# Two attentions and two mixture layers on one core: late normalisation spread out, roots inside head 14's values, two prepared pieces further apart, GpSimd behind the first rows

## The chip, the cores and the metric

One core of one Trainium2 chip. The metric is the device time of one launch in microseconds; less is better.

## The reference, cut to what matters

The input x has 4 batches of 512 rows of 512 numbers. Four layers are added to it in turn, each on a normalised copy:

```python
x = x + attn_a(layernorm(x), w_in, w_out)          # 16 heads of 128, causal
x = x + ffn(layernorm(x), gate_w, w1, b1, w2, b2, shared...)   # 8 experts, top 2, and a shared one
x = x + attn_b(layernorm(x), Wqa, Wqb, Wkva, Wkvb, Wo)         # latent attention
x = x + ffn(layernorm(x), ...)

def layernorm(x): return (x - mean) / sqrt(var + 1e-5)
def attn_a(x, w_in, w_out):
    q, k, v = split(x @ w_in.T)                    # per head
    p = softmax(causal(q @ k.T / sqrt(128)))
    return concat_heads(p @ v) @ w_out.T
```

The change lies in the first line alone.

## The kernel before, in words

Every matrix product is done in three TensorE passes on a high part and a low part of both operands (`product`): ScalarE copies a value into its rounded high part, and VectorE or GpSimd subtracts that from the value to get the low part. So each tile goes TensorE, ScalarE, VectorE and back to TensorE.

The first attention runs in two passes (g = 0 with batches 0 and 1, g = 1 with batches 2 and 3), in each 16 heads h, in each head two steps i, one per batch. Each engine has its own instruction list in program order (`attend_tensor`, `attend_scalar`, `attend_vector`, `attend_gpsimd`, `attend_sync`) and waits on semaphores; there is no planner. `over_heads` writes head pair 0 and head pair 7 out and loops over pairs 1 to 6. A step is a pipeline over three (head, batch) units: it projects query, key and values of the present one, takes mask, maximum and exponentials of the one before (u) and turns and multiplies its probabilities, and adds the output of the one before that (v). Heads 1 to 14 (`not edge(h)`) form query and key of both batches from seven half products, m1 to m7, over sums of the inputs; heads 0 and 15 do them plainly. Both heads' values of a pair are projected together in the even head, in two halves (`project_v`, `values_hi`, `values_lo`), each half with its own PSUM bank, which m7 and m4 of the same step (or m1 and m6 of the next) need again.

What else is woven in:

- Input sums. At the beginning of a pass GpSimd rebuilds the plain inputs (`rebuild_first`, `rebuild_second`), VectorE and GpSimd form four sums (`input_sums`, `third_sum`), ScalarE rounds them (`sums_hi`) and VectorE and GpSimd take the low parts (`sums_lo`). Head 1's half products need them.
- Normalisation. Batch 0 is normalised ahead of the attention, batch 1 inside head 0 of pass 0 (`woven_first`: TensorE turns a tile, ScalarE and VectorE split it). Batches 2 and 3, and then batches 0 and 1 for the next layer, are the late batches (`late_batch`): they are measured in step 0 of head 14 (`measure`: four statistics, four aggregates and the variance for each batch, then five small Newton instructions for each), ScalarE takes the roots there (`roots`), GpSimd makes the rows, and head 15 turns them.
- Pieces. 24 blocks of weights of the later layers are split ahead of time (`prepare`): SP loads one, ScalarE makes the high part, GpSimd the low part, and SP waits for that and stores both. There is one buffer: the load of piece j waits until piece j - 1 is stored. `pieces_of` says in which step a piece is done; pieces 15 and 16 stand in the two steps of head 1 in pass 1, pieces 17 to 23 in the second step of each later even head.
- The SP queue in a head: the next head's query and key weights (after GpSimd has taken the low parts of the present ones), its output weights, in even heads the values' weights, then the head's pieces.

The functions that build the norm and hand `measure` to the attention stand in `program`, in the blocks of VectorE and ScalarE.

Of the kernel before, what the change touches and what calls it, by code (L numbers as in the profile page):

```python
# [314 lines left out]
def pieces_of(g, pair, odd, i):  # L315

    begins = isinstance(pair, int) and pair == 0
    if g == 0:
        return [2 * pair + odd - 1] if i and (odd or not begins) else []
    if begins:  # L320
        return [H - 1 + i] if odd else []
    return [H + pair] if i and not odd else []
# [328 lines left out]
def attend_scalar(nc, act, m, n, a, first=nothing, roots=nothing, prepare=nothing):  # L651
# [55 lines left out]

    def values_hi(g, h, i):
        for half in range(2):
            act.wait_ge(a.v_done, 2 * (H * g + h) + 2 * i + half + 1)  # L710
            for other in range(2):
                nc.scalar.activation(values_part(values_of(m, other, i)[HI], half), values_bank(m, half, other),  # L712
                                     ACT.Copy).then_inc(a.v_hi, 1)

    def sums_hi(g):
        act.wait_ge(a.x_summed, 6 * g + 2)
        nc.scalar.activation(sum_place(m, HI, g, 2), plain_sum(m, LO, g, 2), ACT.Copy).then_inc(a.sum_hi, 1)
        nc.scalar.activation(sum_place(m, HI, g, 1), plain_sum(m, LO, g, 1), ACT.Copy).then_inc(a.sum_hi, 1)
        act.wait_ge(a.x_summed, 6 * g + 3)
        nc.scalar.activation(sum_place(m, HI, g, 4), plain_sum(m, LO, g, 4), ACT.Copy).then_inc(a.sum_hi, 1)  # L720
        act.wait_ge(a.rebuilt, 6 * g + 5)
        nc.scalar.activation(sum_place(m, HI, g, 3), plain_sum(m, LO, g, 3), ACT.Copy).then_inc(a.sum_hi, 1)
# [6 lines left out]
    def step(g, pair, h, odd, i, n1, new=True, hook=nothing):  # L729
# [61 lines left out]
        if n1:  # L791
            output_hi(u)
        if new and not odd:
            values_hi(g, h, i)
        if new and edge(h) and not odd and g == 1 and i == 0:
            sums_hi(g)
        if new:
            for j in pieces_of(g, pair, odd, i):
                prepare(j)
        if new and i == 0 and isinstance(h, int) and h == H - 2:  # L800
            roots(g)
        hook(i, 3)
# [11 lines left out]

def attend_vector(nc, dve, m, n, a, first=nothing, measure=nothing):

# [107 lines left out]
    def step(g, h, odd, i, n1, n2, new=True, hook=nothing):  # L924
# [55 lines left out]
        elif not odd:  # L980
# [9 lines left out]
            if g == 0 and i:  # L990
                input_sums(g)
            add((2, 3))
        else:
# [11 lines left out]
        if new and edge(h) and not odd and g == 1 and i == 0:  # L1005
            input_sums(g)
        if new and edge(h) and not odd:
            values_lo(g, h, i, (0,))
            if i:
                sums_lo(g, (2, 1))  # L1010
            values_lo(g, h, i, (1,))
        elif new and not odd:
            values_lo(g, h, i, (0, 1))
        if new and i == 0 and isinstance(h, int) and h == H - 2:
            measure(g)
        hook(i, 3)
# [12 lines left out]
def attend_gpsimd(nc, pool, m, n, a, prepare=nothing, use_tables=nothing):  # L1029
# [47 lines left out]
    def rebuild_first(g):  # L1077
        if g:
            pool.wait_ge(a.proj_done, 4 * H * g)
        pool.wait_ge(n.xt_lo, NT * (2 * g + 1))  # L1080
        rebuild(g, plain_sum(m, HI, g, 3), 2 * g, 0)
        rebuild(g, plain_sum(m, HI, g, 4), 2 * g, 1)
# [6 lines left out]
    def third_sum(g):  # L1089
        pool.wait_ge(a.x_summed, 6 * g + 2)  # L1090
        pool.wait_ge(a.rebuilt, 6 * g + 4)
        third = plain_sum(m, LO, g, 3)
        nc.gpsimd.tensor_tensor(third, plain_sum(m, HI, g, 3), third, ALU.subtract).then_inc(a.rebuilt, 1)
        pool.wait_ge(a.sum_hi, 4 * g + 4)
        nc.gpsimd.tensor_tensor(sum_place(m, LO, g, 3), third, sum_place(m, HI, g, 3).bitcast(F32),
                                ALU.subtract).then_inc(a.rebuilt, 1)
# [10 lines left out]
    def head(g, pair, odd):  # L1107
# [23 lines left out]
        if edge(h) and not odd and g == 0:  # L1131
            third_sum(g)
        if odd and coming:
            rest_vw(*coming)
        if isinstance(h, int) and h == H - 2:
            late_rows(g, 0, (0, 1))
        for i in range(2):
            for j in pieces_of(g, pair, odd, i):
                prepare(j)

    rest_ahead(0, 0)
    rest_vw(0, 0)
# [1548 lines left out]
def program(nc, x_in, wa, wva, woa, wb, wob, rope, gate, b1, wr, b1r, b2r, b2s, table, out):  # L2691
    with ExitStack() as ctx:
# [117 lines left out]
        m.rank = sb("rank", [P, GT])  # L2810
        m.esc, m.first, m.ids = sb("esc", [P, TILES]), sb("first", [P, 2]), sb("ids", [P, IDS], U32)
        m.picked = [sb("picked0", [P, GT + 1, E], BF16), sb("picked1", [P, NT + 1, E], BF16)]
        m.tri16, m.ones16 = sb("tri16", [P, P], BF16), sb("ones16", [P, P], BF16)
# [102 lines left out]

        def woven_first(stats, start, tile):

            def first(b, i):
# [3 lines left out]
                for t in ((), (0,), (1, 2), (3,))[i] if b == 0 and i >= 0 else ():  # L2923
                    tile(1, t)
            return first

# [41 lines left out]
        def _(dve):  # L2968
# [28 lines left out]

            def measure(g):
                for i in range(2):
                    if g == 0:  # L3000
                        dve.wait_ge(x_loaded[2 + i], 16)
                    norm_measure_vector(nc, dve, m, n, *late_batch(g, i))
                for i in range(2):
                    norm_newton_vector(nc, dve, m, n, *late_batch(g, i))

            attend_vector(nc, dve, m, n, a1, woven_first(stats(0), start(0), tile(0)), measure)
            dve.wait_ge(small_loaded, SMALL)

# [118 lines left out]
```

## Time and profile before

| | us |
|---|---|
| median of three runs | 2427.64 (2424.67 to 2428.95) |
| the profiled execution | 2426.1 |
| its span | 2423.9 |
| TensorE busy in it | 2276.9 (94%) |
| VectorE busy | 1826.9 (75%) |
| ScalarE busy | 1206.4 (50%) |
| GpSimd busy | 935.8 (39%) |

The first attention takes the first 1055 us or so of the span. PE is TensorE, PEld its weight loads, DVE VectorE, ACT ScalarE, POOL GpSimd, SP the engine that issues the loads. A row of the timeline has start, duration, engine, line, operation, what is written and read, and, if the engine was idle before it, in brackets how long and what released it. PEclk is the TensorE clock granted in a stretch, as a share of 2.4 GHz: 1.00 is that level and 0.50 the lower one, 1.2 GHz.

### The profile page before, as it was taken

The numbers are of one execution on the slowest core, as the hardware profiler recorded it, in microseconds if no ns is written. First come the engines' busy times: TensorE is split into PE (matmuls) and PEld (weight loads), VectorE is DVE, ScalarE is ACT, GpSimd is POOL, SyncE is SP. The second block draws the span as 40 slices with busy tenths as digits, with TensorE's granted clock in tenths as the row PEclk, the third lists the DMA queues.
The fourth block names the chain that finished last, engine by engine and source line by source line (L and its number), as shares of the span: only waits on it lengthen the run. The fifth ranks groups of instructions, "written<-read, shape, count | busy, mean of one in ns | idle before, by whom it ended". The sixth has DMA issues, their size and how long they took to land. (4 is left out here: it accounts for less than half of the span.)

```text
span 2423.9 us, 41931 instructions
## 1 busy us (share of the span) xinstructions
PE 2276.9 (94%) x12798; PEld 1953.5 (81%) x12798; DVE 1826.9 (75%) x4044; ACT 1206.4 (50%) x2803; POOL 935.8 (39%) x757
## 2 busy tenths in 40 slices
PE   6999999989899999888999789999999999889997
PEld 5888888878788888767887568888888888767886
DVE  6877777767677777766666749999999999875666
ACT  3555555555455555542332446666666666542334
POOL 5444444365344444345221333333334334234223
PEclk9999999999999999999999899999999999999999
DMA  3455555532533333226884100000000000017866
GB/s 124 168 194 194 194 194 194 194 119 91 210 114 114 114 114 114 81 82 227 300 274 179 58 19 1 19 19 0 18 18 18 0 18 18 18 62 271 282 232 232
DMA packets 106768, 296.61 MB, mean 122 GB/s; under 512 B 9481, under 2 KB 11913, under 8 KB 101025
## 3 DMA queue, kind: packets, MB, share of 16 engines
q1 hardware_dynamic: 85792, 239.59, 28.4%
q0 software_dynamic: 11360, 37.76, 4.1%
q10 hardware_dynamic: 9504, 17.85, 2.2%
q8 instruction: 61, 1.00, 0.2%
q14 instruction: 51, 0.41, 0.1%
HBM read 150.18 MB, written 144.98 MB: 122 GB/s over the span
## 5 line engine op out<-in xcount | busy, mean ns | idle before, releaser
L74 PE MATMUL bank<-wo_hi,hq_hi 128*128 128x512 f32 x576 | 235.5, 409 | 14.7 <-DVE x L1439 13.0
L74 PE MATMUL bank<-xT_hi,w_hi 128*128 128x512 f32 x584 | 236.1, 404 | 10.8 <-DVE xT_lo L1693 4.3
L76 PE MATMUL bank<-xT_hi,w_lo 128*128 128x512 f32 x584 | 232.4, 398 | 0.0
L75 PE MATMUL bank<-xT_lo,w_hi 128*128 128x512 f32 x584 | 232.2, 398 | 0.0
L76 PE MATMUL bank<-wo_hi,hq_lo 128*128 128x512 f32 x576 | 226.6, 393 | 0.0
L75 PE MATMUL bank<-wo_lo,hq_hi 128*128 128x512 f32 x576 | 226.4, 393 | 0.0
L1509 POOL TENSOR_TENSOR qf<-ra,rb 64x512 f32<-64x512 f32 x64 | 82.4, 1287 | 334.1 <-DVE rb L1612 333.9
L831 DVE SCALAR_TENSOR_TENSOR x<-bank,inv,x 128x512 f32<-128x512 f32 x256 | 179.8, 743 | 19.8 <-PE bank L76 19.8
L1357 ACT ACTIVATE s<-s,top 128x128 f32<-128x128 f32 (+3 forms) x256 | 141.0, 552 | 96.6 <-DVE top L1431 96.4
L1439 DVE SCALAR_TENSOR_TENSOR x<-bank,inv,x 128x512 f32<-128x512 f32 x256 | 180.0, 743 | 3.7 <-PE bank L76 0.7
L842 DVE TENSOR_TENSOR hq_lo<-bank,hq_hi 128x512 fp32r<-128x512 f32 (+1 forms) x144 | 80.3, 567 | 130.1 <-ACT arena L712 67.2
L672 ACT ACTIVATE s<-s,top 128x128 f32<-128x128 f32 (+3 forms) x256 | 140.9, 552 | 56.8 <-DVE top L822 56.8
L1033 POOL TENSOR_TENSOR w_lo<-w_raw,w_hi 128x512 fp32r<-128x512 f32 x64 | 82.5, 1290 | 210.0 <-ACT w_hi L648 210.0
L74 PEld LDWEIGHTS bank<-wo_hi,hq_hi 128*128 128x128 f32 x576 | 109.2, 190 | 53.6 <-DVE x L1439 26.3
L74 PEld LDWEIGHTS bank<-xT_hi,w_hi 128*128 128x128 f32 x584 | 112.6, 193 | 37.6 <-DVE xT_lo L192 8.7
L76 PEld LDWEIGHTS bank<-xT_hi,w_lo 128*128 128x128 f32 x584 | 112.0, 192 | 24.5
L75 PEld LDWEIGHTS bank<-xT_lo,w_hi 128*128 128x128 f32 x584 | 112.3, 192 | 24.1
L76 PEld LDWEIGHTS bank<-wo_hi,hq_lo 128*128 128x128 f32 x576 | 109.0, 189 | 24.0
L838 DVE TENSOR_TENSOR pt_lo<-bank,pt_hi 128x384 fp32r<-128x384 f32 (+1 forms) x192 | 104.6, 594 | 31.0 <-ACT pt_hi L678 30.9
L76 PE MATMUL bank<-pt_hi,hq_lo 128*128 128x256 f32 (+2 forms) x384 | 124.6, 324 | 0.0
L75 PE MATMUL bank<-pt_lo,hq_hi 128*128 128x256 f32 (+2 forms) x384 | 124.3, 324 | 0.0
L74 PE MATMUL bank<-pt_hi,hq_hi 128*128 128x256 f32 (+2 forms) x384 | 124.1, 323 | 0.0
(338 smaller groups left out, 7315.9 us busy)
## 6 DMA issues: line engine op xcount, KB each, us to landing
sorted_x<-blank SPq DMA_DIRECT2D x48, 1584.0 KB, 11.6
arena<-split_w SPq DMA_DIRECT2D x32, 1024.0 KB, 5.8
split_w<-arena SPq DMA_DIRECT2D x48, 512.0 KB, 3.5
w_raw<-dram_wa SPq DMA_DIRECT2D x32, 512.0 KB, 5.0
raw<-dram_wr SPq DMA_DIRECT2D x24, 512.0 KB, 5.6
wo_raw<-dram_woa SPq DMA_DIRECT2D x32, 256.0 KB, 4.2
ctok<-dram_wva SPq DMA_DIRECT2D x16, 512.0 KB, 5.1
arrived<-routed_y SPq DMA_DIRECT2D x8, 1024.0 KB, 8.0
```

What stands on the lines that cost most here:

```text
L74: nc.tensor.matmul(out, hi, mov_hi, start=first, stop=False)
L75: nc.tensor.matmul(out, hi, mov_lo, start=False, stop=False)
L76: return nc.tensor.matmul(out, lo, mov_hi, start=False, stop=last)
L672: nc.scalar.activation(at, at, ACT.Exp, bias=m.top[:, slot, t:t + 1], scale=-1.0, accum_out=m.rowsum[:, slot, t:t + 1]).then_inc(a.probs_r ...
L831: nc.vector.scalar_tensor_tensor(out=xt, in0=m.bank[6 + t % 2][:, :], scalar=m.inv[:, slot, t:t + 1], in1=xt, op0=ALU.mult, op1=ALU.add).t ...
L838: nc.vector.tensor_tensor(m.pt_lo[:, dst:dst + cols], m.bank[src][:, 0:cols], m.pt_hi[:, dst:dst + cols].bitcast(F32), ALU.subtract).then_ ...
L842: return nc.vector.tensor_tensor(out, whole, hi.bitcast(F32), ALU.subtract).then_inc(done, 1)
L1033: nc.gpsimd.tensor_tensor(lo, whole, hi.bitcast(F32), ALU.subtract).then_inc(a.w_lo, 1)
L1357: nc.scalar.activation(at, at, ACT.Exp, bias=m.top[:, odd, t:t + 1], scale=-1.0, accum_out=m.rowsum[:, odd, t:t + 1]).then_inc(a.probs_rea ...
L1439: nc.vector.scalar_tensor_tensor(out=xt, in0=m.bank[6 + t % 2][:, :], scalar=m.inv[:, odd, t:t + 1], in1=xt, op0=ALU.mult, op1=ALU.add).th ...
L1509: nc.gpsimd.tensor_tensor(m.qf[HALF:P, :], m.ra[HALF:P, :], m.rb[HALF:P, :], ALU.add).then_inc(a.rope_added, 1)
```

## The change

It moves work between places in the program and adds two waits and one small instruction:

- In each pass one late batch is measured in head 0 (in pass 0 in step 0, in pass 1 in step 1), only the other in head 14.
- In step 0 of head 14 ScalarE takes the roots ahead of the first half of the values, and a one-column exponential between the halves; VectorE does the first Newton step and the other measurement ahead of the values and the second Newton step between their halves.
- The third sum's rounding (`third_hi`) goes behind the values of step 1 of head 0, its low part (`third_lo`) on GpSimd behind the next head's weights. In pass 0 VectorE takes the low part of the second sum earlier, and that of the first behind the values.
- Piece 15 goes from head 1 to step 1 of head 0.
- GpSimd waits for the first two rows of batch 0 before its first weights and for the first two of batch 1 before its first rebuild.

```diff
@@ pieces_of
     if begins:
-        return [H - 1 + i] if odd else []
+        return [H - 1 + odd] if i else []
@@ attend_scalar
-    def values_hi(g, h, i):
-        for half in range(2):
-            act.wait_ge(a.v_done, 2 * (H * g + h) + 2 * i + half + 1)
-            for other in range(2):
-                nc.scalar.activation(values_part(values_of(m, other, i)[HI], half), values_bank(m, half, other),
-                                     ACT.Copy).then_inc(a.v_hi, 1)
+    def values_hi(g, h, i, half):
+        act.wait_ge(a.v_done, 2 * (H * g + h) + 2 * i + half + 1)
+        for other in range(2):
+            nc.scalar.activation(values_part(values_of(m, other, i)[HI], half), values_bank(m, half, other),
+                                 ACT.Copy).then_inc(a.v_hi, 1)
...
+    def third_hi(g):
         act.wait_ge(a.rebuilt, 6 * g + 5)
         nc.scalar.activation(sum_place(m, HI, g, 3), plain_sum(m, LO, g, 3), ACT.Copy).then_inc(a.sum_hi, 1)
...
+        before_last = new and i == 0 and isinstance(h, int) and h == H - 2
+        if before_last:
+            roots(g)
         if new and not odd:
-            values_hi(g, h, i)
+            values_hi(g, h, i, 0)
+            if before_last:
+                nc.scalar.activation(m.exp_set[:, 0:1], m.root[:, 0, 0:1], ACT.Exp)
+            values_hi(g, h, i, 1)
         if new and edge(h) and not odd and g == 1 and i == 0:
             sums_hi(g)
+        if new and edge(h) and not odd and i:
+            third_hi(g)
         if new:
             for j in pieces_of(g, pair, odd, i):
                 prepare(j)
-        if new and i == 0 and isinstance(h, int) and h == H - 2:
-            roots(g)
@@ attend_vector
             if g == 0 and i:
                 input_sums(g)
+                sums_lo(g, (2,))
+            if g == 1 and i:
+                dve.wait_ge(a.y_added, NT * (v + 1) - NT)
+                measure(g, 0)
             add((2, 3))
...
-        if new and edge(h) and not odd:
+        before_last = new and i == 0 and isinstance(h, int) and h == H - 2
+        if before_last:
+            newton(g, 0)
+            measure(g, 1)
+        if new and not odd:
             values_lo(g, h, i, (0,))
-            if i:
+            if edge(h) and i and g:
                 sums_lo(g, (2, 1))
+            if before_last:
+                newton(g, 1)
             values_lo(g, h, i, (1,))
-        elif new and not odd:
-            values_lo(g, h, i, (0, 1))
-        if new and i == 0 and isinstance(h, int) and h == H - 2:
-            measure(g)
+            if edge(h) and i and not g:
+                sums_lo(g, (1,))
@@ attend_gpsimd
     def rebuild_first(g):
         if g:
             pool.wait_ge(a.proj_done, 4 * H * g)
+        else:
+            pool.wait_ge(n.normed, NT + 2)
         pool.wait_ge(n.xt_lo, NT * (2 * g + 1))
...
+    def third_lo(g):
+        third = plain_sum(m, LO, g, 3)
         pool.wait_ge(a.sum_hi, 4 * g + 4)
...
         if edge(h) and not odd and g == 0:
             third_sum(g)
+        if edge(h) and not odd:
+            third_lo(g)
         if odd and coming:
             rest_vw(*coming)
...
+    pool.wait_ge(n.normed, 2)
     rest_ahead(0, 0)
     rest_vw(0, 0)
     use_tables()
@@ program, woven_first
                 for t in ((), (0,), (1, 2), (3,))[i] if b == 0 and i >= 0 else ():
                     tile(1, t)
+                if b == 0 and i == 1:
+                    measured()
@@ program, VectorE's block
-            def measure(g):
-                for i in range(2):
-                    if g == 0:
-                        dve.wait_ge(x_loaded[2 + i], 16)
-                    norm_measure_vector(nc, dve, m, n, *late_batch(g, i))
-                for i in range(2):
-                    norm_newton_vector(nc, dve, m, n, *late_batch(g, i))
-
-            attend_vector(nc, dve, m, n, a1, woven_first(stats(0), start(0), tile(0)), measure)
+            def measure(g, i):
+                if g == 0:
+                    dve.wait_ge(x_loaded[2 + i], 16)
+                norm_measure_vector(nc, dve, m, n, *late_batch(g, i))
+
+            def newton(g, i):
+                norm_newton_vector(nc, dve, m, n, *late_batch(g, i))
+
+            attend_vector(nc, dve, m, n, a1, woven_first(stats(0), start(0), tile(0), lambda: measure(0, 0)), measure, newton)
```

## Rows read from the trace of the kernel before

**Rows 1.** Stretches: length, busy time and count by engine, PEclk, DMA share, GB/s.

```profile
30.00:35.00 5.00, 4.46 (x19) 4.07 (x20) 3.25 (x6) 0.60 (x1) 0.71 (x1) 0.50 0.24 91
...
400.00:480.00 80.00, 80.00 (x482) 71.54 (x481) 59.01 (x125) 41.61 (x100) 33.26 (x26) 1.00 0.59 205
480.00:520.00 40.00, 33.40 (x194) 29.67 (x193) 28.74 (x77) 19.54 (x45) 18.79 (x10) 0.91 0.32 110
```

**Rows 2.** Timeline of pass 0, head 14, steps 0 and 1; columns as told above.

```profile
474.49 0.60 ACT L706 ACTIVATE hq_hi<-bank 128x512 fp32r<-128x512 f32 x1 [0.42 <-PE bank L76]
476.03 0.68 DVE L842 TENSOR_TENSOR hq_lo<-bank,hq_hi 128x512 fp32r<-128x512 f32 x1
480.85 1.28 ACT L198 ACT_TABLE_LOAD   x1
481.20 0.41 DVE L842 TENSOR_TENSOR arena<-bank,arena 128x256 fp32r<-128x256 f32 x1
481.53 2.46 DVE L145 BATCH_NORM_STATS2 stats<-x 128x6 f32<-128x512 f32 x4
487.24 0.17 DVE L158 RECIPROCAL rstd<-root 128x4 f32<-128x4 f32 x1
490.17 0.26 DVE L822 CUSTOM_DVE_ANT_0 s<-bank,mask 128x128 f32<-128x128 f32 x1
492.82 2.39 PE L393 MATMUL bank<-ident,s 128*128 128x128 f32 x10 [6.60 <-ACT s L672]
497.14 0.42 PE L76 MATMUL bank<-wo_hi,hq_lo 128*128 128x512 f32 x1
```

**Rows 3.** Timeline of TensorE in pass 1, head 14, step 1.

```profile
1012.12 2.18 PE L393 MATMUL bank<-ident,s 128*128 128x128 f32 x9 [6.60 <-ACT s L672]
```

**Rows 4.** Timeline of pass 1, head 0, step 1: ScalarE, TensorE and VectorE.

```profile
558.97 1.06 ACT L722 ACTIVATE xT_hi<-xT_lo 128x1024 fp32r<-128x1024 f32 x1 [0.58 <-POOL xT_lo L1093]
...
562.26 1.31 PE L393 MATMUL bank<-ident,s 128*128 128x128 f32 x10 [1.85 <-ACT s L672]
...
571.92 1.41 DVE L831 SCALAR_TENSOR_TENSOR x<-bank,inv,x 128x512 f32<-128x512 f32 x2 [4.23 <-PE bank L76]
```

**Rows 5.** Timeline of pass 1, heads 0 to 2; last row: issues, to landing in us.

```profile
568.88 0.33 SPq L1148 DMA_DIRECT2D w_raw<-dram_wa  x1
...
592.00 0.62 ACT L648 ACTIVATE arena<-w_raw 128x512 fp32r<-128x512 f32 x1
...
601.98 2.86 POOL L1583 TENSOR_TENSOR arena<-raw,arena 128x1024 fp32r<-128x1024 f32 x1
608.73 0.34 SPq L1558 DMA_DIRECT2D raw<-dram_wr  x1
612.88 1.06 ACT L1572 ACTIVATE arena<-raw 128x1024 fp32r<-128x1024 f32 x1 [10.35 <-DMA raw<-dram_wr]
616.68 1.11 PE L393 MATMUL bank<-ident,s 128*128 128x128 f32 x4 [7.14 <-ACT s L672]
...
w_raw<-dram_wa SPq DMA_DIRECT2D x3, 512.0 KB, 5.4
```

**Rows 6.** Timeline of pass 0, the start and head 0, step 0.

```profile
8.72 1.25 DVE L164 TENSOR_SCALAR newt<-newt 128x4 f32<-128x4 f32 x1
20.70 5.85 DVE L150 TENSOR_SCALAR var<-moments 128x4 f32<-128x4 f32 x1
21.75 4.70 POOL L1075 TENSOR_TENSOR xT_hi<-xT_hi,xT_lo 128x1024 f32<-128x1024 f32 x2
30.18 1.11 PE L214 MATMUL bank<-ident,xn 128*128 128x128 f32 x4 [4.24 <-DVE xn L174]
42.80 0.43 PE L74 MATMUL bank<-xT_hi,w_hi 128*128 128x512 f32 x1
```

**Rows 7.** Timeline of TensorE in pass 0, head 1, step 0.

```profile
61.21 0.47 PE L74 MATMUL bank<-xT_hi,w_hi 128*128 128x512 f32 x1 [1.88 <-issue]
...
70.47 0.78 PE L74 MATMUL bank<-xT_hi,arena 128*128 128x512 f32 x1 [0.84 <-DVE u2s L856]
```

More of the change, by code:

```diff
@@ L812, in attend_scalar, with attend_vector @@
     step(PASSES, 0, 0, 0, 0, True, new=False)
-def attend_vector(nc, dve, m, n, a, first=nothing, measure=nothing):
+def attend_vector(nc, dve, m, n, a, first=nothing, measure=nothing, newton=nothing):
     def mask_and_max(u, slot):
@@ L2811, in program @@
         m.esc, m.first, m.ids = sb("esc", [P, TILES]), sb("first", [P, 2]), sb("ids", [P, IDS], U32)
+        m.exp_set = sb("exp_set", [P, 1])
         m.picked = [sb("picked0", [P, GT + 1, E], BF16), sb("picked1", [P, NT + 1, E], BF16)]
@@ L2915, in program, with woven_first @@
         later = {(b + 1, t): (b, t) for b in range(B - 1) for t in range(NT)}
-        def woven_first(stats, start, tile):
+        def woven_first(stats, start, tile, measured=nothing):
             def first(b, i):
```

## The prediction, made before the changed kernel was run

> **What bounds the kernel now.** I read the profile from the wide view inward. The stretch view first: between 400 and 480 us TensorE is busy for the whole 80 us at full granted clock, while VectorE has 21 us to spare; between 480 and 520 us TensorE is busy for only 33.4 of 40 us, at a mean clock of 0.91 [rows 1]. So the first attention, up to about 1055 us, is bound by TensorE, and only its holes can be won. Next I walked the timeline of TensorE and noted each hole over 0.3 us. Up to 1050 us those that the change can touch are: 4.24 us at 26, four small ones between 59 and 71 (the first 1.88, the last 0.84), 6.60 at 486, 1.85 at 560, 7.14 at 610 and 6.60 at 1006. Behind the long ones the clock stands at its lower level (1.2 instead of 2.4 GHz), so a hole costs more than its length. What follows the first attention waits for it as a whole; I let it shift rigidly.
>
> **Head 14, both passes (the largest part).** Today VectorE finishes the low halves of the values at 481.6, then measures two batches (481.53 to 487.24, so 2.86 us each) and takes two Newton steps (to 490.1, 1.4 us each, of which 0.8 once is a wait). Only then comes the mask of the next step at 490.17, and TensorE's transposes of the probabilities follow it 2.65 us later, at 492.82, after 6.60 us idle [rows 2]. TensorE then runs at the lower clock until 497.14, 4.3 us, in which it does 2.15 us of full-speed work: 2.2 us more. So the place costs 8.8 us.
>
> After the change one measurement is gone from here, and the other work sits in front of the values, where VectorE waits for TensorE anyway. I place it on the same clock. ScalarE's copy of the output ends at 475.1, the square-root table takes 1.28 us, the first root is there at 476.6. VectorE's last row before it ends at 476.7 [rows 2]; Newton for the first batch 1.0 (to 477.7), measurement of the second 2.86 (480.6), root 0.2 (480.8). ScalarE copies the first half of the values (0.7, 481.5), loads the exponential's table (1.28) and does the one-column exponential (0.2 with its start, 483.1), and copies the second half (0.7, 483.8). VectorE: low parts of the first half 482.3, second Newton 483.3, low parts of the second half 484.6, mask at 484.75. That is 5.4 us earlier than 490.17, and the transposes come at 487.4. Who waits for what was put in: TensorE's product m7 needs the first half's low parts, at 482.3 instead of the 481.9 at which it gets there, 0.4 us; behind that it has work to 486.7, and 0.7 us is left before the transposes. Two holes of half a microsecond should not lower the clock (the 1.85 us hole at 560 didn't), so the 2.2 us go too: 7.6 us. Pass 1 shows the same hole, 6.60 us at 1012.12 [rows 3], so twice: **15.2 us**. Bounds: 6.0 and 8.3 each. The measurement that left, of batch 2 in head 0 of pass 0, is costed with the start; that of batch 0 in head 0 of pass 1 goes between the key's low part, which ends at 567.7, and an addition that VectorE takes up at 571.92 after 4.23 us idle [rows 4]: 2.86 us fit, cost nothing, and would cost at most their length if that wait vanished.
>
> **Pieces 15 and 16.** The 7.14 us hole at 610: TensorE waits for ScalarE's exponentials, ScalarE has been held 10.35 us at the copy of piece 16 by its load, issued only at 608.73, because the SP queue stands until GpSimd has taken piece 15 (601.98 to 604.84) and its store has landed [rows 5]. With piece 15 one head earlier, its load goes out near 551 (behind the values' load of head 0); ScalarE copies the third sum and then the piece behind head 0's values, until 578, GpSimd does the third sum and the piece, 2.4 us each, until 582; the store is done by 587, and piece 16 lands before 595; ScalarE asks for it at 602.5. The hole goes, 7.14, and the clock's loss behind it: the restart at 616.68 has the look of the one in head 14, I take 1.9. **9.0 us** (8.5 to 9.5). What is queued behind the moved step: on SP the weight load of head 2, now at 568.88, must wait for GpSimd's piece 15 and goes out near 583; it lands 5.4 us later, at 588.3; GpSimd's weight sums then run to about 592, and ScalarE's copy of them is due at 592.00 [rows 5]. Just in time, nothing charged; if late, it costs microsecond for microsecond. ScalarE gets the third sum and piece 15 (1.06 each) ahead of head 1's exponentials: 0.4 us on the first product's way, charged below.
>
> **Third sum, pass 1.** ScalarE's copy of the third sum waits for GpSimd until 558.97 and holds the exponentials; TensorE loses 1.85 us at 562.26 [rows 4]. Taken out, the exponentials follow the mask, and 0.3 us is left. 1.6 less the 0.4 above: **1.2 us** (0.5 to 1.6).
>
> **The start.** What is queued behind the two waits put in: on GpSimd behind the first the low weights of head 0 (needed by TensorE's first product, after 16 us; done by 13), behind the second the rebuilds, head 0's output weights and head 1's weight sums; on SP the loads that wait for these, now at 27.7, go out some 3 us later and are needed after 46. None is on the path. Here VectorE and GpSimd get into each other's way. A four-column instruction at 8.72 takes 1.25 us while GpSimd works on weights, and the variance of batch 1, again four columns, starts at 20.70 and ends at 26.55, when GpSimd's two rebuilds (21.75 to 26.45) are over; such an instruction alone takes 0.17, as the reciprocal in head 14 [rows 2, 6]. The rows of batch 1 come late, TensorE idles 4.24 us until 30.18 and is then at the lower clock (0.50 from 30 to 35) [rows 1, 6]. With both new waits GpSimd's rebuilds start only behind the first two rows of batch 1; the variance is ready 4.7 us earlier (GpSimd's short table work until 21.8 still stands in its way), so the first row comes by 25.4, before TensorE asks at 25.9, and with Newton undisturbed both are there at 24. Won: 4.24, a further 0.35 behind the transposes, 2.4 for the half-speed products from 31.65 to 36.5, and 1.1 of the 2.1 us that the first rows wait at 8.72 (the rest I give back: GpSimd's two products now fall on rows 3 and 4). Given back: the rebuilds now run from 24 to 29 and hold VectorE's third row of batch 1 (0.2 at TensorE), the moved measurement of 2.86 us delays the fourth row and the tiles behind it (1.0), and the last low part before the second batch's projection, which starts at 42.80 now, comes 0.6 after TensorE's scores. 8.1 less 1.8: **6.3 us** (2.5 to 8.0).
>
> The Trainium skill, "SBUF — State Buffer", section "Who interferes with whom", says that VectorE and GpSimd arbitrate for one port pair and that the loser blocks for the other's whole instruction. By that the third row of batch 1 is held by one rebuild at most, the 0.2 above; the row at 20.70, which outlasted three GpSimd instructions, says that it can be held through a whole run of them, 4.6 us, and gives 2.5 instead of 6.3. Rule and trace agree on the block, not on its length.
>
> **Heads 0 and 1, pass 0.** TensorE restarts at 61.21 and 70.47 out of small holes [rows 7]. ScalarE no longer waits for the third sum before the output's copy, and one 1.2 us subtraction goes from between the value halves and one in front of the addition. But that one meets GpSimd's third sum. If GpSimd goes first I get 0.3 us, if not about 5 with the clock's part; nearest is the row at 20.70, so I take **2.2 us**.
>
> **Sum.** 15.2 + 9.0 + 1.2 + 6.3 + 2.2 = 33.9 us. The profiled execution took 2426.1 us (span 2423.9), so 2392.2; the median of the three runs, 2427.64, is 1.5 above it: **2393.7 us**.
>
> **Rivals.**
> - GpSimd holds VectorE at the start as at 20.70: 2.5 and 0.3 instead of 6.3 and 2.2, and some of the lower clock remains. 28.2 won, 2399.4. For it: the one row of that length. Against: every other wait of a small instruction ended with one GpSimd instruction. 17%.
> - The values of head 14 come too late. They stand behind a root that waits for VectorE and behind a table load; if TensorE's holes there add up to some 3 us and the clock falls, each pass wins 3.5 us less: 2400.7. For it: my chain has 0.4 us of room in it. Against: no row in it is unknown. 9%.
> - Piece 15 only moves the hole: the weights of head 2 land late, and TensorE stands 5 us and runs slow for 2: 2400.7. For it: that load is 14 us later. Against: the middle heads live with the same order. 7%.
> - Slower: the piece's chain on SP stays behind in pass 1. If in head 2 and each later even head the raw load is issued as late as at 608.73, each of the seven pieces 17 to 23 costs another 9 us, 63 in all: 2393.7 + 63 = 2457. It makes the kernel slower from the fourth such piece on (34 / 9). Against: TensorE runs these heads now without a hole, and their pieces don't move. 2%.
> - The change doesn't do what it says (the holes close and open elsewhere for the same sum): within 0.2%. 3%.
>
> **How the numbers follow.** The forecast holds 60%, with its own range 2387 to 2398; the rest, 2%, is a larger gain. The likeliest total stands. All best bounds together (8.3 twice, 9.5, 1.6, 8.0, 5) give 40.7, 2387; all worst 23.8 (12.0, 8.5, 0.5, 2.5, 0.3), 2404. The range 2386 to 2405 takes in the first three rivals. A measurement of this kernel can tell about 0.2%, 5 us. Faster by more: 60 + 17 + 9 + 7 + 2 = 95%; within 3%; slower 2%.
>
> **What would show it.** Right: head 14 without a hole over 1 us and with the mask some 8 us after the output's low part; no wait of ScalarE for the raw load over 1 us in pass 1; clock 1.00 around 490, 615 and 1010; batch 1's variance in 1.2 us or less and projection of the second batch near 36.5. Wrong: a TensorE hole behind the weight sums of head 2, one in front of product m7 or m4 of head 14, or VectorE's rows of batch 1 held through several GpSimd instructions. I would be most wrong if full-speed TensorE, with its holes closed, met a limit of VectorE or ScalarE that the holes hide.

## The result and the profile after

The changed kernel takes 2387.27 us (median of 6 runs, 2385.52 to 2390.32) where the kernel before took 2424.08 (6 runs, the three told above and three beside the changed kernel, 2414.89 to 2428.95): a ratio of 0.985, with a 95% interval of 0.983 to 0.986. It is faster by 37 us. Its profiled execution took 2386.49 us, 39.6 less than that of before (2426.1). The first lines of its page:

```profile
span 2384.4 us, 41934 instructions
...
PE 2264.1 (95%) x12798; PEld 1942.9 (81%) x12798; DVE 1818.9 (76%) x4044; ACT 1206.0 (51%) x2805; POOL 939.5 (39%) x757
```

TensorE has the same 12798 products and is busy 12.8 us less: holes do not count as busy, so this part is mostly the lower clock behind them. The rest of the gain is idle time. The stretches that answer to [rows 1], and those in which the long holes lay before (length, busy time and count of PE, PEld, DVE, ACT and POOL, PEclk, DMA share, GB/s), changed kernel:

```profile
30.00:35.00 5.00, 4.14 (x33) 3.81 (x31) 4.97 (x15) 2.46 (x5) 1.73 (x3) 1.00 0.42 156
...
70.00:75.00 5.00, 5.00 (x26) 4.10 (x25) 3.99 (x13) 3.55 (x11) 3.52 (x3) 1.00 0.60 219
...
485.00:490.00 5.00, 5.00 (x36) 4.60 (x35) 2.95 (x13) 3.10 (x8) 2.11 (x1) 1.00 0.02 3
...
610.00:615.00 5.00, 5.00 (x40) 4.87 (x40) 2.56 (x5) 1.13 (x3) 0.00 (x0) 1.00 0.01 3
...
1010.00:1015.00 5.00, 5.00 (x30) 4.31 (x29) 3.30 (x7) 2.45 (x6) 0.00 (x0) 1.00 0.20 58
```

The clock is 1.00 in all of them. In the kernel before, the stretch 70:75 shows what a lower clock looks like:

```profile
70.00:75.00 5.00, 4.53 (x13) 3.66 (x14) 2.49 (x5) 0.49 (x2) 2.92 (x5) 0.66 0.75 227
```

To see where the 39.5 us of span came from, I took the start of the same TensorE instruction in both timelines at places between the edits. The gain grows like this:

| place on TensorE | before | after | gained so far |
|---|---|---|---|
| first projection | 18.06 | 16.51 | 1.6 |
| projection of the second batch | 42.80 | 35.19 | 7.6 |
| head 1, product m5 | 70.47 | 60.87 | 9.6 |
| output products behind it | 76.30 | 65.08 | 11.2 |
| pass 0, behind head 14's transposes | 497.40 | 478.30 | 19.1 |
| pass 1, head 0, transposes | 562.26 | 541.54 | 20.7 |
| pass 1, head 1, product m5 | 582.33 | 561.81 | 20.5 |
| behind the transposes of [rows 5] | 620.83 | 591.33 | 29.5 |
| last step of the first attention | 1059.06 | 1021.88 | 37.2 |
| end of the span | 2423.9 | 2384.4 | 39.5 |

### The profile page after: what moved, and what is told of

Same layout as the page of the kernel before. It is cut to its first block and busy times, and to the rows that moved or that the text cites. A ratio compares the mean times of both kernels' runs of the same rounds, so it can differ in the third digit from the quotient of the medians.

```text
span 2384.4 us, 41934 instructions
## 1 busy us (share of the span) xinstructions
PE 2264.1 (95%) x12798; PEld 1942.9 (81%) x12798; DVE 1818.9 (76%) x4044; ACT 1206.0 (51%) x2805; POOL 939.5 (39%) x757
## 5 line engine op out<-in xcount | busy, mean ns | idle before, releaser
L74 PEld LDWEIGHTS bank<-xT_hi,w_hi 128*128 128x128 f32 x584 | 112.1, 192 | 36.8 <-DVE xT_lo L192 8.8
L75 PEld LDWEIGHTS bank<-xT_lo,w_hi 128*128 128x128 f32 x584 | 111.6, 191 | 23.8
L75 PEld LDWEIGHTS bank<-wo_lo,hq_hi 128*128 128x128 f32 x576 | 108.8, 189 | 17.1
```

What stands on the lines that cost most here:

```text
L74: nc.tensor.matmul(out, hi, mov_hi, start=first, stop=False)
L75: nc.tensor.matmul(out, hi, mov_lo, start=False, stop=False)
```

## The experiments

"The last step" below is the last row but one of that table: TensorE at the last step of the first attention. From there to TensorE's last product the same code took between 1345.1 and 1351.1 us in the fourteen profiles of this study, so an experiment with a single execution is read at this place and not by its time.

**Piece 15 alone.** The kernel before with one line changed.

```diff
-        return [H - 1 + i] if odd else []
+        return [H - 1 + odd] if i else []
```

> The kernel before with one line changed: piece 15 in step 1 of head 0 and piece 16 in step 1 of head 1 of pass 1. Theory (the hole of 7.14 us at 610 and 1.9 us of lower clock behind it are nothing but the late load of piece 16): TensorE's first matmul of head 1, step 0's second half and all after 620 come 9.0 us earlier, everything before 582 is unmoved, the time is 9 us less, ratio 0.9963. Rival (the hole moves to the weights of head 2, which now load 14 us later): a TensorE hole of 3 us or more appears between 590 and 600 and the gain is 4 us or less.

2416.29 us (2412.19 to 2419.69), a ratio of 0.9961 [0.9948, 0.9973] to 2426.02 of before. TensorE at the head 0 and head 14 transposes of pass 1:

```profile
560.87 1.31 PE L393 MATMUL bank<-ident,s 128*128 128x128 f32 x10 [1.87 <-ACT s L672]
...
1002.00 2.40 PE L393 MATMUL bank<-ident,s 128*128 128x128 f32 x10 [6.60 <-ACT s L672]
```

Between them lie 441.13 us, against 449.86 in the kernel before [rows 3, 4]: 8.7 us for the piece, hole and clock together, and the holes of the other terms are still there. TensorE has no hole over 0.3 us between these two places, so the rival (the hole moves to the weights of head 2) fell.

**GpSimd's two waits alone.** The kernel before with both waits and nothing else.

```diff
+        else:
+            pool.wait_ge(n.normed, NT + 2)
...
+    pool.wait_ge(n.normed, 2)
```

> The kernel before with GpSimd's two new waits alone. Theory (the start is lost to VectorE standing behind GpSimd): the variance of batch 1 takes 0.2 to 1.2 us instead of 5.85, the 4.24 us hole and the lower clock behind it go, and the projection of the second batch starts 8 to 9 us earlier than 42.80, because no moved measurement is in the way (the changed kernel has it 7.6 earlier); 8.5 us less in all, ratio 0.9965. Rival (the gain of the start comes as much from the other edits around head 0): 4 us or less here.

2415.78 us (2412.44 to 2418.08), ratio 0.9956 [0.9939, 0.9973]. The projection of the second batch comes 8.5 us earlier (34.33), the last step 9.6. VectorE's rows of batch 1:

```profile
21.78 1.00 DVE L174 TENSOR_SCALAR xn<-x,moments,rstd 128x512 f32<-128x512 f32 x2
25.33 2.56 DVE L174 TENSOR_SCALAR xn<-x,moments,rstd 128x512 f32<-128x512 f32 x1
```

Two rows pass in 1.00 us, and the third is held by one rebuild, as the forecast had it. Product m5 comes at 61.96, 8.5 earlier as well. The last 1.1 us come behind it, where the clock was low in the profile of before; that low clock was chance, not the waits' doing (see heads 0 and 1 below).

**Each wait taken out of the changed kernel.** First the one ahead of the first weights.

```diff
-    pool.wait_ge(n.normed, 2)
```

> The changed kernel without GpSimd's wait for the rows of batch 0. Theory: two of VectorE's four-column instructions stand behind one GpSimd instruction each again (1.2 us instead of 0.17), and the first projection starts 1.5 us later, at 18.0; all later marks of the first attention are 1.5 us later. Rival (TensorE has slack behind it): the projection of the second batch is unmoved.

VectorE's Newton step is held again and the first projection falls back by 1.7 us, to 18.19. VectorE:

```profile
8.85 1.25 DVE L164 TENSOR_SCALAR newt<-newt 128x4 f32<-128x4 f32 x1
```

The second projection is 1.8 us later (36.98) and the last step 2.0 (1023.83), so TensorE has no slack behind it: the rival fell. Then the one ahead of the rebuilds.

```diff
-        else:
-            pool.wait_ge(n.normed, NT + 2)
```

> The changed kernel without GpSimd's wait for the rows of batch 1. Theory (a small instruction of VectorE can be held through a run of GpSimd instructions): a variance or Newton step of batch 1 takes over 4 us once, TensorE has its hole of 4 us in front of batch 1's first tile and the lower clock behind it, second batch's projection at 42 instead of 35.2: 6 to 7 us more. Rival (one GpSimd instruction at a time, as the Trainium skill's page on SBUF has it): each of VectorE's small instructions waits for one rebuild at most, 2.4 us, but there are several; the hole is under 2.5 us and the loss 3 us or less.

The long hold came back, now on the first row of batch 1 instead of the variance. VectorE, GpSimd and TensorE:

```profile
20.38 7.51 DVE L174 TENSOR_SCALAR xn<-x,moments,rstd 128x512 f32<-128x512 f32 x2
...
20.22 1.27 POOL L2918 TENSOR_TENSOR b<-b 8x512 f32<-8x512 f32 x1
21.46 4.69 POOL L1089 TENSOR_TENSOR xT_hi<-xT_hi,xT_lo 128x1024 f32<-128x1024 f32 x2
...
26.54 0.66 PE L214 MATMUL bank<-ident,xn 128*128 128x128 f32 x4 [2.61 <-DVE xn L174]
```

A row takes 0.5 us, so of 7.51 us for two the wait is 6.5. The transposes that need the first of them start at 26.54, so that one came out only behind both rebuilds (26.15). The projection of the second batch comes at 40.02 (4.8 us later), the last step at 1026.76 (4.9 later). The direction is the theory's, the size lies between theory and rival. In all three profiles without this wait (before, piece 15 alone, this one) an instruction of VectorE is held for 5.8 us or more here; in the eleven with it, none takes over 2.6 us.

**Head 14 as before.** The changed kernel with the old order in head 14 and both late batches measured there.

```diff
-            if g == 1 and i:
-                dve.wait_ge(a.y_added, NT * (v + 1) - NT)
-                measure(g, 0)
...
-        if before_last:
-            newton(g, 0)
-            measure(g, 1)
...
+        if before_last:
+            measure(g, 0)
+            measure(g, 1)
+            newton(g, 0)
+            newton(g, 1)
...
-                if b == 0 and i == 1:
-                    measured()
```

On ScalarE `roots(g)` is behind the values again, without the exponential.

> The changed kernel with head 14 as it was (both measurements, both Newton steps and both roots behind the values, no small exponential), nothing measured in head 0. Theory: the two holes of 6.6 us with 2.2 us of lower clock each are back, 7.8 us a pass, less 1 us that the measurement costs at the start: 14.5 us more than the changed kernel, about 21 to 22 less than before, ratio to before 0.991. Rival (the clock has no part in it, it is the holes alone): 6.4 us a pass and 12 more than the changed kernel.

2405.35 us (2403.4 to 2405.47), ratio 0.9915 [0.9898, 0.9932]. TensorE:

```profile
480.48 2.39 PE L393 MATMUL bank<-ident,s 128*128 128x128 f32 x10 [6.60 <-ACT s L672]
...
989.24 2.40 PE L393 MATMUL bank<-ident,s 128*128 128x128 f32 x10 [6.60 <-ACT s L672]
```

Both holes of 6.60 us are back to the hundredth, and the last step is 14.4 us later. Without the measurement in head 0 its start is 1.1 us earlier (34.05), so head 14 is worth 15.5.

**Only the order in head 14 as before.** One measurement stays in head 0; ScalarE's roots are behind the values, without the exponential.

```diff
-        if before_last:
-            newton(g, 0)
-            measure(g, 1)
...
+        if before_last:
+            measure(g, 1)
+            newton(g, 0)
+            newton(g, 1)
```

> The changed kernel with only the order in head 14 put back (measurement, Newton and roots behind the values); the other measurement stays in head 0. Theory (work is what delays the mask, so taking one measurement away gives 2.86 us of the 6.3, and hiding the rest in the gap gives the other half): a TensorE hole of 2.5 to 3.5 us in front of the transposes in each pass, 5 us more than the changed kernel if the clock stays up behind it and 9 if it falls. Rival (the order is everything, taking one measurement away gives nothing by itself): holes of 5 us or more, 13 us more than the changed kernel.

2398.17 us (2394.76 to 2399.93), ratio 0.9888 [0.9871, 0.9904]. TensorE:

```profile
476.49 2.34 PE L393 MATMUL bank<-ident,s 128*128 128x128 f32 x10 [3.77 <-ACT s L672]
...
982.11 2.39 PE L393 MATMUL bank<-ident,s 128*128 128x128 f32 x10 [3.77 <-ACT s L672]
```

So the measurement that left took 2.83 us of the hole, its own length, and the new order 3.5 more. Ten transposes take 2.34 us here and 1.31 at full clock: a hole of 3.77 us brings the lower clock too. The last step is 6.85 us later although the start was 2.35 earlier (by chance: the code of the start is that of the changed kernel, but the third row was not held), so the order is worth 9.2 of the 15.5 us, and the moved measurements are worth 6.3, before what the one in pass 0 costs at the start (1.1).

**Without the one-column exponential.**

```diff
-            if before_last:
-                nc.scalar.activation(m.exp_set[:, 0:1], m.root[:, 0, 0:1], ACT.Exp)
```

> The changed kernel without the one-column exponential between the values' halves. Theory (ScalarE loads the exponential's table by itself ahead of the first exponential, while it waits for the mask, as before in this place at 488.11): no loss, the second half's copies come 1.5 us earlier and the transposes in head 14 come at the same time or 0.2 us earlier. Rival (the table load then falls on the path): the exponentials start after mask plus 1.28 us, and each pass loses 1 us or more.

I expected no loss; each head 14 lost 0.5 us (transposes at 476.02 after 0.81 us idle). VectorE, GpSimd, ScalarE:

```profile
471.22 1.16 DVE L164 TENSOR_SCALAR newt<-newt 128x4 f32<-128x4 f32 x1
...
471.07 1.29 POOL L1045 TENSOR_TENSOR w_lo<-w_raw,w_hi 128x512 fp32r<-128x512 f32 x1 [13.36 <-ACT w_hi L648]
...
471.01 1.28 ACT L672 ACT_TABLE_LOAD   x1
473.68 0.40 ACT L672 ACTIVATE s<-s,top 128x128 f32<-128x128 f32 x1 [1.39 <-DVE top L826]
```

The table load itself is hidden here: the first exponential waits 1.39 us more for the mask. But ScalarE reaches the weight split earlier, GpSimd's low part therefore starts at 471.07 instead of 472.84, and VectorE's small instruction is held for it (1.16 instead of 0.17). So the load between the value halves is worth having, by these rows because it keeps GpSimd out of VectorE's Newton step, not because it hides the load. That was in neither theory.

**The second sum's low part between the value halves again, pass 0.**

```diff
-                sums_lo(g, (2,))
...
-            if edge(h) and i and g:
-                sums_lo(g, (2, 1))
+            if edge(h) and i:
+                sums_lo(g, (2, 1) if g else (2,))
```

> The changed kernel with the low part of the second sum of pass 0 between the values' halves again, where it stood before. In the changed kernel it takes 3.3 us (1.2 alone) because it stands behind GpSimd's third sum, and holds the output's and the values' low parts. Theory: the hole of 1.27 us in front of head 1's first product shrinks to 0.5 or less, head 1 then waits a little longer for the second bank, and head 1's later marks come 0.3 to 1 us earlier. Rival (VectorE is the bound there, the order doesn't matter): no change at the marks behind head 1, or later ones.

```profile
52.20 0.47 PE L74 MATMUL bank<-xT_hi,w_hi 128*128 128x512 f32 x1 [0.25 <-issue]
59.23 1.31 PE L393 MATMUL bank<-ident,s 128*128 128x128 f32 x10 [2.66 <-ACT s L672]
```

One hole closes (0.25, was 1.27) and the next opens by as much (2.66, was 1.33). Product m5 comes at 61.39 (60.87 before this edit). The last step is 0.6 us later, 0.3 of it from the start. The rival held: in the changed kernel VectorE is busy for 13.9 of the 14 us from 46 to 60. Here it is busy for 11.7 of them, but GpSimd's third sum still takes 3.4 us, so the collision stays. That this is why the place of the low part hardly matters is argued, not shown.

**More rows ahead of the rebuilds.** The second wait at `NT + 3`, then at `NT + 4`.

```diff
-            pool.wait_ge(n.normed, NT + 2)
+            pool.wait_ge(n.normed, NT + 3)
```

> The changed kernel with GpSimd's second wait for three rows of batch 1 instead of two. In the changed kernel the third row is issued at 25.43, in the middle of a rebuild, and ends at 27.68. Theory (GpSimd's rebuild is all that holds it, and GpSimd has 3.5 us idle behind this stretch): the third row takes 0.55 us, the holes of 0.56 and 0.86 us at 28 and 32 shrink, and the second batch's projection starts 1.5 to 2.5 us earlier than 35.19, with all later marks of the first attention. Rival (the moved measurement and the fourth row bound this stretch): 0.5 us or less, because the fourth row is then held instead.

The third row is no longer held (25.90, 0.54 us), but the rebuilds now meet what follows on VectorE, and TensorE waits 1.84 us instead of 0.86 for the fourth row's tiles:

```profile
29.73 1.54 DVE L150 TENSOR_SCALAR var<-moments 128x4 f32<-128x4 f32 x1
31.19 1.57 DVE L174 TENSOR_SCALAR xn<-x,moments,rstd 128x512 f32<-128x512 f32 x1
```

The last step is 0.9 us later (1022.74).

> The changed kernel with GpSimd's second wait for all four rows of batch 1. Theory: neither the third nor the fourth row is held, the second batch's projection starts near 32.5, but GpSimd starts its rebuilds 6 us later and its work up to head 1's weights ends 3 to 4 us later than 44.65; the weights are needed from 51, so the marks of heads 0 and 1 gain as much as the start, 2 to 3 us. Rival (GpSimd's list becomes the bound): the input sums wait for GpSimd's last rebuild, and what is won at 33 is lost again at head 1's first product.

No row is held and the second batch is projected at 33.04, 2.2 us earlier, but then GpSimd is late with everything behind it, and more than the gain is lost:

```profile
29.59 4.77 POOL L1089 TENSOR_TENSOR xT_hi<-xT_hi,xT_lo 128x1024 f32<-128x1024 f32 x2 [8.27 <-DVE xn L174]
...
54.70 0.77 PE L74 MATMUL bank<-xT_hi,w_hi 128*128 128x512 f32 x1 [5.15 <-issue]
```

The last step is 1.4 us later (1023.26). Two rows is the best of the three, by one profile each. With the changed kernel's start the second projection came between 34.9 and 35.5 us in five profiles and at 32.84 in a sixth, so the loss with three rows (35.93) is little more than this spread; the 5.15 us hole with four rows is far outside it.

**A better version: the third sum later.** In pass 0 GpSimd forms the third sum not behind the first two of VectorE's three input sums, but behind all three and the low part of the second: that is the count of four.

```diff
-        pool.wait_ge(a.x_summed, 6 * g + 2)
+        pool.wait_ge(a.x_summed, 6 * g + (2 if g else 4))
```

> The changed kernel with GpSimd's third sum of pass 0 waiting until VectorE has the low part of the second sum (a count of 4 instead of 2 on the same semaphore). In the changed kernel the two meet and the low part takes 3.3 us. Theory (the meeting is what holds heads 0 and 1): the low part takes 1.2 us, the hole of 1.27 us at head 1's first product shrinks to 0.5 or less, the mask of head 1 comes 2 us earlier, and the marks behind head 1's m5 come 1.5 to 2 us earlier. Rival (moving the third sum only moves the meeting to the low part of the first sum): under 0.7 us.

In the changed kernel VectorE's low part of the second sum and GpSimd's third sum collide:

```profile
47.06 3.45 POOL L1109 TENSOR_TENSOR xT_lo<-xT_hi,xT_lo 128x1024 f32<-128x1024 f32 x1 [2.42 <-DVE xT_lo L914]
...
48.28 3.32 DVE L848 TENSOR_TENSOR xT_lo<-xT_lo,xT_hi 128x1024 fp32r<-128x1024 f32 x1
```

With the later sum:

```profile
48.51 1.23 DVE L848 TENSOR_TENSOR xT_lo<-xT_lo,xT_hi 128x1024 fp32r<-128x1024 f32 x1
...
49.82 2.41 POOL L1109 TENSOR_TENSOR xT_lo<-xT_hi,xT_lo 128x1024 f32<-128x1024 f32 x1 [4.94 <-DVE xT_lo L848]
```

Each takes its own length again (1.23 and 2.41 us), m5 comes at 59.20 instead of 60.87, and the last step 1.9 us earlier (1020.02). In seven profiles with the third sum as in the changed kernel, the changed kernel's own among them, the way from the second projection to m5 takes 25.7 us; here it takes 23.8. The single time, 2388.24, does not show the gain, so the same kernel was timed in five executions. (The expectation calls the count of four "four input sums"; it is three sums and one low part.)

> The changed kernel with GpSimd's third sum of pass 0 behind VectorE's first four input sums instead of its first two, as in the single look before, now timed in five rounds. Theory: that look had TensorE at the last step of the first attention 1.86 us earlier than the changed kernel (1020.02 against 1021.88), though its start was 0.2 later; the first attention binds through TensorE, so the whole moves by that: about 2385.4 against the changed kernel's median of 2387.27, a ratio of 0.983 to 0.985 to the kernel before, and the last step of the first attention between 1019 and 1022. The difference to the changed kernel is less than a timing of 0.2% can tell for sure. Rival: the clock behind the hole at 1292 and the chance at the start (2 us either way) are larger than the gain; then the median is within 1 us of 2387.3 or above it. If it is above 2389, the gain at the mark is lost further back, and the theory that the whole moves rigidly is wrong for it.

2386.0 us (2384.56 to 2386.36), ratio 0.9833 [0.9819, 0.9846] to the kernel before, last step 1020.17 (1.7 earlier), and again 23.8 us from the second projection to m5. Against 2387.27 the median is 1.3 lower, and the intervals of the two ratios overlap. The gain is shown at the last step in two profiles; in the time it is likely, not shown.

## Why the prediction was right, term by term

The forecast was 2393.7 us with a range of 2386 to 2405. The time, 2387.3, is inside, near the lower end, and "faster" held.

| term | forecast | measured at TensorE |
|---|---|---|
| head 14, both passes | 15.2 | 7.9 + 7.7 = 15.6 |
| pieces 15 and 16 | 9.0 | 9.0 |
| third sum, pass 1 | 1.2 | 1.6 - 0.2 = 1.4 |
| start | 6.3 | 7.6 |
| heads 0 and 1, pass 0 | 2.2 | 3.6, of it 1.6 chance |
| sum | 33.9 | 37.2 |

Each is the growth between two places of the first table. Profile against profile, 39.6 us were won where 33.9 were forecast. Of the 5.7 us more, 1.7 are the terms' own: start 1.3, head 14 0.4, third sum 0.2, heads 0 and 1 less 0.2. Another 1.6 in heads 0 and 1 are the clock, by chance (below), and 2.3 lie behind the first attention, where the code is the same, also by chance: 1.6 us were lost at its last step, 2.8 won at 1303, the rest in small steps. Without these two the changes are worth 35.6 us. The 39.6 are not the gain of the medians either, which is 36.8: the forecast started from a median of 2427.64, but with the three runs beside the changed kernel the median of before is 2424.08, and 3.6 of the 6.4 us by which the time lies below the forecast are this.

**Head 14: right in mechanism and size.** The chain as it ran in pass 0:

```profile
463.28 0.60 ACT L706 ACTIVATE hq_hi<-bank 128x512 fp32r<-128x512 f32 x1 [0.42 <-PE bank L76]
463.90 1.28 ACT L198 ACT_TABLE_LOAD   x1
...
466.44 2.48 DVE L145 BATCH_NORM_STATS2 stats<-x 128x6 f32<-128x512 f32 x4
...
470.20 1.28 ACT L799 ACT_TABLE_LOAD   x1
...
472.69 0.42 DVE L848 TENSOR_TENSOR arena<-bank,arena 128x256 fp32r<-128x256 f32 x1
473.10 0.26 DVE L828 CUSTOM_DVE_ANT_0 s<-bank,mask 128x128 f32<-128x128 f32 x1
```

From the output's copy to the mask were 15.68 us before [rows 2]; now they are 9.82. The forecast had 10.26 on the same clock (474.49 to 484.75), and it wanted the mask some 8 us behind the output's low part (464.82): it is 8.28. It charged TensorE 0.7 us of idle time in front of the transposes; it was 0.26 us in pass 0 and 0.31 in pass 1, and m7 waited 0.16 where 0.4 was charged. The rival "the values come too late" fell. The moved measurement in head 0 of pass 1 was hidden as told: VectorE's idle time before the addition went from 4.23 us [rows 4] to 1.37.

**Pieces: right.** SP, ScalarE and GpSimd in heads 0 to 2 of pass 1, changed kernel:

```profile
556.15 1.06 ACT L1594 ACTIVATE arena<-raw 128x1024 fp32r<-128x1024 f32 x1
...
562.99 0.73 SPq L1170 DMA_DIRECT2D w_raw<-dram_wa  x1
...
566.88 0.33 SPq L1580 DMA_DIRECT2D raw<-dram_wr  x1
...
568.12 0.84 POOL L1080 TENSOR_TENSOR w_raw<-w_raw 128x256 f32<-128x256 f32 x1 [3.53 <-DMA w_raw<-dram_wa]
...
581.89 1.05 ACT L1594 ACTIVATE arena<-raw 128x1024 fp32r<-128x1024 f32 x1
```

Piece 16's load is issued at 566.88 and ScalarE's copy at 581.89 has no wait, where it had 10.35 us [rows 5]. The weights of head 2, which I had called just in time, land at 568.1, and the split that needs GpSimd's sums runs at 570.51: in time, with GpSimd's 3.53 us wait as the only trace. My working stands on the clock of the kernel before: I had SP issue that load near 583; less the 20 us won by then this is 563, which is what the row shows. The rival of this term fell, as did the slower one: no later piece's load was late.

**Third sum: right.** The transposes wait 0.23 us instead of 1.85; heads 0 and 1 then give back 0.2 where 0.4 was charged.

**Start: right mechanism, term too small by 1.3.** The two waits did what the forecast says: the variance of batch 1 takes 0.17 us (at 19.15), and the held third row is there. VectorE and TensorE, changed kernel:

```profile
21.57 1.01 DVE L174 TENSOR_SCALAR xn<-x,moments,rstd 128x512 f32<-128x512 f32 x2
...
25.43 2.25 DVE L174 TENSOR_SCALAR xn<-x,moments,rstd 128x512 f32<-128x512 f32 x1
28.43 0.63 PE L214 MATMUL bank<-ident,xn 128*128 128x128 f32 x4 [0.55 <-DVE xT_lo L192]
32.76 0.63 PE L214 MATMUL bank<-ident,xn 128*128 128x128 f32 x4 [0.86 <-DVE xT_lo L192]
```

Third and fourth row cost TensorE 0.55 and 0.86 us, 1.4 together, where 1.2 was charged. What was set too low is what was won: the first projection came 1.55 us earlier, where I had counted 1.1. The rest of the difference also lies in front of the second projection (35.19, where I wanted 36.5), and I cannot split it further. Two profiles of the old start differ by 0.6 us there (42.80, and 43.44 with piece 15 alone), so part of it can be chance. The rival "GpSimd holds VectorE as at 20.70" fell for the changed kernel, and taking the second wait out brought it back at 4.9 us. With the wait it is in none of eleven profiles, without it in all three: the wait, not luck, keeps it away.

The Trainium skill, "SBUF — State Buffer", section "Who interferes with whom", has the loser blocked for one whole instruction. In the changed kernel and with the waits alone the third row is held by one rebuild, as the page says. Without the second wait, and before at 20.70, it is held through three instructions, longer than the page says. One instruction of GpSimd is therefore no safe bound for the wait. In each of these cases GpSimd went on without a pause when VectorE got in, behind the second rebuild (at 26.42 before, at 27.35 in the changed kernel), so VectorE does not have to wait for the end of the whole run either.

**Heads 0 and 1: right in size, and 1.6 us of luck on top.** Of the 3.6 us, 2.0 come before m5 (7.6 to 9.6 gained), close to the 2.2, and 1.6 behind it: the stretch 70:75 was at 0.66 before and is at 1.00 now. The change did not do that. With piece 15 alone all code up to here is that of the kernel before, and TensorE has the same four small holes, of 1.87, 1.50, 0.93 and 0.85 us (before: 1.88, 1.50, 0.94 and 0.84, [rows 7] has the first and last), but the clock stayed up behind them (the kernel before has 0.78 us for this product, at 70.47):

```profile
71.08 0.50 PE L74 MATMUL bank<-xT_hi,arena 128*128 128x512 f32 x1 [0.85 <-DVE u2s L856]
```

From m5 to the output products are 5.83 us in the profile of before and 4.2 in the thirteen others, that one included. The forecast gave this clock no term; that it came out in the forecast's favour is luck of the one profile of before. The 0.85 us in front of m5 is still there, but the 1.88 us hole in front of m1 [rows 7] is 1.27. The waits alone gave nothing before m5 (27.6 us from the second projection, as before; 25.7 in the changed kernel). The place of the second sum is worth 0.2 at m5; third sum and first sum were not moved alone, and which of them gives the other 1.8 stays open. The collision I feared (0.3 if GpSimd goes first) did happen, 3.32 us for a low part of 1.23. It cost about 1.9 us, which is what the later third sum wins back.

## What to carry to other kernels

A short VectorE instruction on the way to TensorE should be kept clear of a run of GpSimd instructions, not just of one: let GpSimd wait for it, and move GpSimd's wait by as many instructions as its own list has room for and no further (two rows won, four lost more than they won). Statistics and roots that nobody needs yet belong in front of a copy that waits for TensorE anyway; here even a table load between two such copies was worth having (0.5 us a pass). When terms of one engine's holes are added up, give each the clock behind it as a part of its own: here it was a fifth to a quarter of what each long hole cost. Behind the holes of 0.8 to 2.9 us told below it came or not with the same code, so a single profile can hold a loss, or miss one, that no change made.

## What the runs showed of the hardware that was not expected

**The same hole, another clock.** At the end of the first mixture layer TensorE waits 2.86 or 2.87 us in every profile for the same VectorE instruction. The product behind it, changed kernel (in the kernel before it stands at 1330.79):

```profile
1294.67 0.47 PE L74 MATMUL bank<-w2b_hi,hq_hi 128*128 128x512 f32 x1 [2.87 <-DVE x L2266]
```

From there to the next projection the same work took 11.75 us before (clock 0.50 in 1330:1335) and 8.94 in the changed kernel (no lower clock). Over the fourteen profiles it is 8.9 to 11.8 us. The holes of 3.77 us and more in head 14 were followed by the lower clock in both passes; those of 1.3 us at 53 and 59 in the changed kernel and of 1.87 at 561 with piece 15 alone were not, though in the kernel before four small ones between 59 and 71 together were (0.66 in 70:75) and the same four with piece 15 alone were not. At the last step of the first attention, with holes of 1.40 and 0.85 us in every profile, the clock fell in three of them (changed kernel, piece 15 alone, second sum between the halves: 8.7 us to the output product) and not in the other eleven (7.2). At 2.87 it went both ways with the same code as well: up to 2.8 us in one execution for nothing the kernel does.

**Statistics run beside GpSimd.** VectorE's four statistics took 2.46 us while GpSimd worked (28.20, changed kernel) and 2.46 us where GpSimd was idle (468.04, with only the order in head 14 as before). With three rows ahead of the rebuilds they ran at 26.96, again in 2.46 us, beside a rebuild, and the four-column variance behind them was held (29.73, 1.54 us). Why an instruction that arrives within the first of three is let in at neither of the two boundaries between them stays open; in the run with only the order in head 14 as before a row issued at 24.65, some 0.2 us ahead of the boundary between the two rebuilds, was let in there (0.54 us).
